# Tower kernel: unit turns by DMA in FFN block 0, down products by parts, block 1's attention rows by DMA

## The reference

```python
h = rms(rms(emb_table[x]) * norm_weight @ proj_weight.T)          # x: 16 x 256 token ids below 128
# attention, 16 heads of 32, on layernorm(h)
q, k = feature_map(u @ Wq.T), feature_map(u @ Wk.T); v = u @ Wv.T
attn = where(causal, (q k^T / sqrt(32)) ** 2, 0)
h = h + ((attn @ v) / (attn.sum(-1) + eps)) @ Wo.T
# FFN with Hadamard transforms (fwht), on layernorm(h)
x = fwht(x * SU_ug) / 64
a = silu(x @ W_gate.T * s_gate) * (x @ W_up.T * s_up)             # 512 -> 2048
h = h + fwht(a * SU_dp) / 64 @ W_down.T * s_down                  # 2048 -> 512
```

## Time and profile before

| | us |
|---|---|
| median of 3 runs | 1368.69 (1368.03 to 1368.8) |
| the profiled execution | 1369.22 |
| its span | 1367.4 |
| start to first `product` of block 0 | 0 to 64.5 |
| block 0's attention heads | 64.5 to 126.8 |
| output product, norm and mixing of block 0's rows | 126.8 to 168.3 |
| FFN block 0, gate and up | 168.3 to 324.1 |
| FFN block 0, down | 324.1 to 380.6 |
| FFN block 1 | 380.6 to 523.5 |
| FFN blocks 2 to 7 | 523.5 to 1367.4 |

### The profile page before, as it was taken

The page is one execution under the profiler, slowest core; times in us unless marked ns, Lnnn a source line. Parts: engine busy times, 40 slices in busy tenths (PEclk is TensorE's granted clock), DMA queues, the critical chain, the costliest instruction groups (busy, mean ns, idle before and its releaser), DMA issues.

```text
span 1367.4 us, 18781 instructions
## 1 busy us (share of the span) xinstructions
PE 1258.8 (92%) x7257; PEld 620.6 (45%) x7257; DVE 658.7 (48%) x1154; ACT 397.9 (29%) x703; POOL 565.2 (41%) x483
## 2 busy tenths in 40 slices
PE   5565398999999999999999999999999999999999
PEld 3453054554444444444444444444444444444444
DVE  2654558782645363545455445534553644361110
ACT  5452354442133212330233113311331133211210
POOL 0443244342266424752375227632664266421210
PEclk9797699999999999999999999999999999999999
DMA  9912313311435234423444244333543445020000
GB/s 307 318 24 62 78 36 65 70 26 37 100 101 109 47 93 108 106 57 85 101 108 70 70 101 108 83 67 90 115 86 55 100 101 108 16 70 24 0 0 31
DMA packets 232708, 113.97 MB, mean 83 GB/s; under 512 B 197893, under 2 KB 215609, under 8 KB 232121
## 3 DMA queue, kind: packets, MB, share of 16 engines
q1 hardware_dynamic: 220160, 74.38, 25.7%
q0 software_dynamic: 11520, 37.76, 9.4%
q10 hardware_dynamic: 952, 0.75, 0.2%
HBM read 57.01 MB, written 9.70 MB: 49 GB/s over the span
## 4 chain that ended last, share of the span: by engine, by line
PE 77%; DVE 9%; DMA 4%; issue 4%; ACT 4%; POOL 1%; SPq 0%; DVEq 0%; POOLq 0%; ACTq 0%
PE bank L1178 23%; PE bank L1179 23%; PE bank L1180 23%; PE bank L1330 3%; DMA prod<-sg 2%; PE bank L1173 2%; DVE wd L568 1%; PE bank L1221 1%; DVE wd L567 1%; DVE wgu L553 1%; DVE prod L765 1%; PE bank L1171 1%; DMA hid<-in_L_tok_norm_weight 1%; PE bank L1339 1%; ACT wgu L951 1%
## 5 line engine op out<-in xcount | busy, mean ns | idle before, releaser
L1178 PE MATMUL bank<-xT,wgu 128*128 128x512 f16 x1024 | 389.8, 381 | 1.4 <-DVE xT L804 1.4
L1179 PE MATMUL bank<-xT,wgu 128*128 128x512 f16 x1024 | 389.8, 381 | 0.0
L1180 PE MATMUL bank<-xT,wgu 128*128 128x512 f16 x1024 | 389.8, 381 | 0.0
L470 POOL TENSOR_TENSOR hid<-a,hid 128x512 f16<-128x512 f32 x128 | 172.9, 1350 | 284.4 <-ACT hid L951 284.1
L839 DVE SCALAR_TENSOR_TENSOR a<-bank,kap,sg 128x512 f32<-128x512 f32 x128 | 96.1, 751 | 313.6 <-PE bank L1180 296.1
L1178 PE MATMUL bank<-wd,hid 128*128 128x512 f16 x512 | 194.1, 379 | 0.0
L1180 PE MATMUL bank<-wd,hid 128*128 128x512 f16 x512 | 194.0, 379 | 0.0
L1179 PE MATMUL bank<-wd,hid 128*128 128x512 f16 x512 | 194.0, 379 | 0.0
L951 ACT ACTIVATE hid<-a 128x512 f16<-128x512 f32 x128 | 80.9, 632 | 278.8 <-DVE a L839 278.8
L1180 PEld LDWEIGHTS bank<-xT,wgu 128*128 128x128 f16 x1024 | 100.5, 98 | 121.9 <-issue 2.0
L1178 PEld LDWEIGHTS bank<-xT,wgu 128*128 128x128 f16 x1024 | 100.8, 98 | 117.7 <-DVE xT L804 2.3
(11 more groups left out here) (192 smaller groups left out, 1371.1 us busy)
## 6 DMA issues: line engine op xcount, KB each, us to landing
out<-a SPq DMA_DIRECT2D x24, 256.0 KB, 2.2
wgu<-in_L_ffn_W_gate SPq DMA_DIRECT2D x16, 256.0 KB, 6.6
wgu<-in_L_ffn_W_up SPq DMA_DIRECT2D x16, 256.0 KB, 5.1
wd<-in_L_ffn_W_down SPq DMA_DIRECT2D x4, 1024.0 KB, 9.3
out<-h_row SPq DMA_DIRECT2D x8, 256.0 KB, 2.0
hid<-att_table,ids_p POOLq DMA_INDIRECT x84, 3.5
xT<-in_L_tok_proj_weight SPq DMA_DIRECT2D x1, 1024.0 KB, 7.3
p<-in_L_attn_Wq SPq DMA_DIRECT2D x1, 1024.0 KB, 11.9
```

The lines of the kernel that those rows point to most:

```text
L470: nc.gpsimd.tensor_tensor(hid[:, 1, s, :], a32[:, :], hid[:, 0, s, :], ALU.subtract)\
L1178: mm(dst, w[0], v[0], start=first, stop=False)
L1179: mm(dst, w[0], v[1], start=False, stop=False)
L1180: return mm(dst, w[1], v[0], start=False, stop=final)
```

## The change

- A gate/up unit is now 128 rows by 512 columns. Units 0 to 11 are still turned by PE, beside block 0's attention, with a ring of three banks. Units 12 to 31 are made in slots 0 to 9 of block 0's FFN, two a slot, without PE: ACT scales the raw unit in place and copies its high part into one of three stage buffers (`RING = 3`), POOL makes the low part there, and SP issues one DMA transpose of both parts into the weights' tile. ACT waits with unit x until the transpose of unit x - 3 has landed.
- Down units go the same way, with DVE making the low part: split in slots 9 to 18, then PE multiplies by the float16 Hadamard matrix (two matmuls) in slots 10 to 22, ACT and DVE split the result.
- Block 0's gate and up have two banks each, as in the other blocks; the down product goes by four parts of the FFN columns, each part for all four row tiles.
- Block 0's attention takes 18 slots and a tail in place of 32. Its own attention rows and FFN input rows are now turned by PE (`o_flip`, `x_flip`) and copied by ACT. For block 1, whose attention runs in block 0's FFN, they stay with the DMA, now in one SP list with the units (`first_block`).
- Four butterfly passes go before block 0's FFN in place of two. The norm weights are loaded ahead of the projection's, the third down tile behind the gate and up weights.
- The value weights' turns move ahead of the score products; Wo's squares and turns move from before the first `product` into slots 4 to 7 and 13 to 16.

```diff
+RING = 3
+TURNED = 12
+UNIT_AT = tuple(range(1, 13))
+UNITS_BESIDE = 10
+DOWN_SQUARES = (3, 3, 3, 3, 2, 2)
+BOUND_BESIDE, FIT_BESIDE = 1, 6
+MIXED_BEFORE = 4
+MIX_BESIDE = (2, 3, 4, 5, 6, 7, 8, 8, 9, 10, 11, 12)
+SPLIT_BESIDE = (9, 10, 11, 13, 13, 13, 14, 14, 14, 15, 15, 15, 16, 16, 17, 18)
+HADA_BESIDE = (10, 11, 12, 14, 14, 15, 15, 16, 16, 17, 18, 18, 19, 20, 21, 22)
+NEXT_AT0 = (11, 13, 15, 17)
+HEADS_AT0 = (4, 8, 12, 16)
+O_AT0 = (5, 9, 13, 16)
+O_FLIP_AT0 = (6, 10, 14, 17)
+def units_beside(s):
+    return [TURNED + 2 * s, TURNED + 2 * s + 1] if s < UNITS_BESIDE else []
...
             def pair(b, s):
...
                 fetch(1, s)
                 feed(0, s)
+                for x in units_beside(s):
+                    unit_low(x)
                 product(1, s)
                 attend(1, s)
...
+            def unit_high(x):
...
+                if x >= TURNED + RING:
+                    act.wait_ge(*landed(x - RING))
...
+                if x < UNITS:
+                    act.wait_ge(S["gu_scaled"], x // 8 + 1)
+                    copy(unit_raw(x), unit_raw(x), scale=unit_scale(x)).then_inc(S["st_scaled"], 1)
+                    act.wait_ge(S["st_scaled"], x - TURNED + 1)
+                    copy(stage_of(x)[:, 0, :], unit_raw(x)).then_inc(S["st_hi"], 1)
...
-                feed(0, s, GATE0)
-                for u in units_beside(2 * s):
-                    unit(u, D_TURN)
...
+                feed(0, s, GATE[s % 2])
+                for x in units_beside(s):
+                    unit_high(x)
+                for v in down_hadas(s - 1):
+                    down_unit(v)
+                for v in down_splits(s):
+                    unit_high(UNITS + v)
                 feed_high(0, s)
...
+            def first_block():
+                for s in range(SUMS_AT[3] + 1):
+                    for x in units_beside(s) + [UNITS + v for v in down_splits(s)]:
+                        unit_turn(x)
+                    for q, m in P_TURN_AT.get(s, ()):
+                        p_turn(1, q, m)
...
+            def tail():
+                for m in range(4):
+                    row_sum(0, m)
+                    if m:
+                        x_low(0, m - 1)
+                    if m > 1:
+                        xT_low(0, m - 2)
+                    row_norm(0, m)
+                    if m == 0:
+                        pair_norm(2)
+                        half_terms(0)
+                    if m == 1:
+                        pair_scale(2)
+                        bound_low(0)
...
+                    if m == 3:
+                        pair_norm(3)
+                xT_low(0, 2)
+                x_low(0, 3)
+                down_mix(MIXED_BEFORE - 1)
+                xT_low(0, 3)
+                pair_scale(3)
...
+            def feed_down_by_parts(s):
+                part, m = (s - FT) // 4, (s - FT) % 4
+                if m == 0:
+                    pe.wait_ge(S["al_done"], 4 * part + 4)
+                    pe.wait_ge(S["d_lo"], 4 * part + 4)
```

More of the change, by code:

```diff
@@ L365, in _ @@
+            for m in range(4):
+                p_turn(1, 0, m)
+            first_block()
+            for b in range(1, NB - 1):
+                block_io(b, b + 1)
+            for m in range(4):
+                store(NB - 1, m)
             sp.wait_ge(S["stored"], 16 * 4 * NB)
@@ L1266, in _, with count @@
                 last.then_inc(S["qk_ready"], 1)
+            def count(n, bank):
+                for i in range(2):
+                    c = SEQ * i
+                    tokens = onehot0 if first(n) else onehot
+                    mm(bank[:, c:c + SEQ], tokens[:, 2 * i, :], cum0, start=True, stop=False)
+                    last = mm(bank[:, c + P:c + SEQ], tokens[:, 2 * i + 1, :], cum1, start=False, stop=True)
+                last.then_inc(S["count_ready"], 1)
+            pe.wait_ge(S["par_land"], PARAMS)
+            pe.wait_ge(S["onehot_ready"], 2)
+            count(0, COUNT0)
+            pe.wait_ge(S["wv_diag"], 2)
+            for u in range(12, 16):
+                small_unit(u)
             def qk_turn(i):
@@ new lines, in attend, with x_flip @@
+                if s in mix_at:
+                    x_mix(n, mix_at.index(s))
+                if s in wo_at:
+                    wo_rows(n, wo_at.index(s))
+            def x_flip(m):
+                pe.wait_ge(S["xl_done"], m + 1)
+                pe.wait_ge(S["xc_done"], m)
+                bank = PICK[0][:, :].bitcast(F16)
+                for i in range(2):
+                    for k in range(DC):
+                        c = (DC * i + k) * P
+                        last = nc.tensor.transpose(bank[:, c:c + P], x16[:, i, k * P:(k + 1) * P], ident16)
+                last.then_inc(S["flip_ready"], 1)
@@ new lines, in wo_rows @@
+            def wo_rows(n, m):
+                if m == 0 and first(n):
+                    pe.wait_ge(S["oT_done"], QUADS)
+                    pe.wait_ge(S["wo_lo"], 4)
+                elif m == 0:
+                    pe.wait_ge(S["oT_land"], 16 * QUADS * n)
+                if m >= 2:
+                    pe.wait_ge(S["h1_done"], 4 * n + m - 1)
+                c = slice(m * P, m * P + P)
+                for k in range(DC):
+                    last = split_mm(WOUT[m % 2][:, :], [oT[:, k, i, c] for i in range(2)],
+                                    [wo_t[:, i, k, :] for i in range(2)], k == 0, k == DC - 1)
+                last.then_inc(S["wo_ready"], 1)
```

1066 lines of the change are left out of this document (567 added, 499 removed).

## The result

The changed kernel takes 1357.8 us, median of 4 runs (1356.54 to 1361.44). The kernel before took 1368.36 beside it. The ratio is 0.9929, 95% interval 0.9907 to 0.9951: faster by 0.7%, where 2.7% were forecast, and the time lies above the forecast's range (1306 to 1350). The profiled execution is the slowest of the four, 1361.44 us with a span of 1359.6, so stages read from it are together 3.6 us longer than in the median.

A forecast was written before the change was run, and what follows sets the result against it. Blocks from 380.6 us on are PE-bound and unchanged; only earlier work moves. First gate at 147 plus 195.8 for FFN block 0 starts block 1 at 342.8, 37.8 earlier: 1369.2 - 37.8 = 1331.4, forecast 1331, range 1306 to 1350.

The forecast's parts named there:

- Up to the first product: Kernel start to block 0's first attention product: starts at 49.5 us in place of 64.5, 15 us gained.
- Block 0's attention: First product to first output product: heads 11.5 us apart, one 18 us stall at POOL's second gather, output product at 107.
- G: Start of FFN block 0's first gate matmul: 147 us, 21 earlier, bounds 138 and 154.
- FFN block 0, slots 0 to 9: First gate to slot 9's `hid<-a`: 94.0 us, with 1.5 charged for passes in six loops and 12 for slot 8.
- The loop of 7.9: FFN block 0's early slots: waiting for a stage buffer's transpose makes one `hid<-a` follow another by 7.9 us.
- the ring has slack: Rival: DVE and POOL don't collide, slots 0 to 9 take 7.9 us or less, second gather not held; 1310 us, chance 0.21.
- slots 10 to 15 and down: Rest of FFN block 0: DVE, then PE, sets the slots; last `a` at 130.5 us, then 65.3 to block 1.
- F: Time from FFN block 0's first gate matmul to block 1's: 195.8 us, 16.5 less, bounds 179 and 209.
- One float32 product goes, 18 matmuls come: 65.3: Last `a` to block 1: 62.3 us before, less 0.9, plus 3.9, gives 65.3.
- By parts, stores bunch, PE hides it: End of FFN block 0: finishes about 3.6 us apart, last store 14 after slot 28, PE needing its bank 15.4 after.
- PE's clock falls: Rival: pauses in each slot drop PE to 1.2 GHz, a slot's work taking 10.4 us; 1346 us, chance 0.18.
- SP's one list: Rival: unit transposes queue behind attention transposes waiting for gathers, four bursts of 13 us; 1383 us, chance 0.04.

The follow-up runs named there:

- e4: The change with POOL's second to fourth gathers for block 1 later in block 0's attention and its tail: 1354.1 us.
- e2: The change with the twelve butterfly passes beside FFN block 0 cut to 16 elements a partition (result not kept): 1345.9 us.
- e7: The change with a ring of four places in place of three for the gate/up units: 1359.9 us.
- e8: The change with POOL's low parts of 20 gate/up units cut to 16 of 512 columns (result not kept): 1346.6 us.
- e3: The change with all down-unit work left out of FFN block 0 (result not kept): 1326.4 us.
- e5: The change with DVE's low parts of down units ahead of block 1's attention row in slots 18, 20 and 22: 1349.3 us.
- e1: The change with the down units' Hadamard products one slot later on PE (slots 11 to 22): 1359.4 us.
- c3: c2 with only the first three Hadamard products of down units one slot later: 1341.1 us.
- c2: The change with the edits of e4 and e5 together: 1345.0 us.
- c4: c2 with down unit 3 taken after 4, 5 and 6, at most two units a slot in slots 9 to 15, Hadamard products rescheduled: 1347.0 us.
- c5: c4 with one of slot 8's two butterfly passes kept there, the others a slot later, and the unit order adapted: 1346.0 us.
- e6: e1 with ACT's scaled halves of down units behind its copies of `a` and of block 1's product: 1361.8 us.
- e9: The change with both the ring of four (e7) and the short POOL low parts (e8): 1347.2 us.

## Why the prediction was wrong, step by step

- **Up to the first product**, 49.5 forecast, 51.83 measured: 2.3 us late. The score products began at 46.4 in place of 45.1 and took 2.1 us in place of 1.1; from their end to the first product it was 3.3, 3.2 forecast. The 15 us gained are 12.7.
- **Block 0's attention.** Heads were to follow at 11.5 (the terms add up to 11.7, a slip); they came at 12.6, 13.7 and 17.0. The stall at POOL's second gather is there, and e4 prices it at 3.1 us. The output product was 7.5 late; the first product is 2.3 of that, and the two distances between heads 3.3. The tail was 38.1, 40 forecast. G is 5.7 over in this execution, 4.9 over by the mean of nine.
- **FFN block 0, slots 0 to 9.** 94.0 forecast, 92.5 measured, and steps of 7.7 to 9.4 in slots 1 to 8. The number was right, in part by luck. The loop of 7.9 is borne out by e2 (8.0 with the passes short). But the 1.5 us charged to each of six loops were about half a microsecond over slots 1 to 8, and the slot with two passes took 13.6 in place of 12; the errors went against each other. "A ring replaces it" is not the whole pace either: with a ring of four the length stays. The rule I quoted from the Trainium skill, SBUF — State Buffer, Who interferes with whom, has the two engines exclude each other for a whole instruction. By that rule 1.5 us a loop looked like a surcharge; the trace agrees with the rule where the two took turns (1.64 and 1.53 for products of 0.69), but a wait can also span several of POOL's instructions: 6.21 us for an operation of 1.22 (e7).
- **The rival "the ring has slack"** is out: ACT stood for landings eight times in the change, and steps 2 and 3 fell to 6.3 once a fourth place was there (e7). That alone brought no time; with POOL's low parts short it was 11 us (e8).
- **The step that failed: slots 10 to 15 and down.** I worked it out as DVE's work in slots 10 to 12 and PE's work in slots 13 to 15, and added the down units as 32 matmuls (7 us) and a low part or two a slot. None of their waits was priced: their transposes behind the ring's in SP's list, their products in PE's list ahead of the next gate, their low parts behind rows in DVE's. Without them, the last `a` comes at 126.2 and F is 185.9 (e3), under the forecast of 130.5 and 195.8. With them, 142.6 and 220.0. They cost 34 us of F (31.4 by the medians), where the forecast had 9.9 above e3's F. The first `a` behind the wait in slot 10, that of slot 11, came at 111.6 in place of 104.8. Of the 24.2 us by which F missed, 11.6 are the low parts behind a row (e5; 8.5 by the medians). The last `a` was 12.1 late, and 9.2 of that go with the Hadamard products a slot later (e1), but e1 gained no time by it, and with the first three alone it was 2.4 of F and 3.9 of the time (c3 against c2). These prices don't add up to the miss by themselves: e2 and e8, which leave the down units alone, each took 13.6 from F as well, so what the ring, the passes and POOL delay, the down units wait for too.
- **"One float32 product goes, 18 matmuls come: 65.3"** for the last `a` to block 1. With DVE's order mended it is 65.9 (e5). The work was counted rightly, the list it stands in was not.
- **By parts, stores bunch, PE hides it**: right to within the 4 us that PE idles there in e3. The distances of 3.6 and 14 us are not shown.
- **PE's clock falls.** It did, 0.84 and 0.91, but as a result. After its 13.44 us of waiting PE made ten matmuls from 256.61 on at 0.43 us each and one at 0.30, some 2.2 us over the faster step, on the path. With fewer waits the clock came back (0.88 and 0.97 in e3). That it is small as a cause is shown for this place only. By the starts in the timelines, about 76 of PE's 512-column matmuls in FFN block 0 stood 0.43 us apart in place of 0.216, where the kernel before has 20 and e3 has 47: some 16 us against 4 and 10. How much of that lies on the path, no run tells.
- **SP's one list**: not as I put it, by gathers. In slot 9 it did matter: the first down unit's transpose stood behind two others, and the four of `p` (5.43 us) held back the second unit's to 259.18, which PE did not notice, as it came to that product at 263.99 only and didn't wait.

What stays open: c3's last `a` is at 138.4, 12.1 us after e3's, with only 5.9 and 2.0 us left as longest waits of its Hadamard products. How much of that is the work of the halves on ACT and DVE, and how much is ring, banks and POOL, c4 and c5 did not tell apart. Nor was it tried to take e1's loss in slot 15 to a cause: e6 only ruled out one order.

## What to carry to other kernels

When work is moved into a stage, cost it by each list that it stands in, not by its own duration: for every operation ask what its engine's list holds behind it while it waits. Here down units with 7 us of matmuls cost 31 to 34, and three lines of order gave 8.5 back. Opening a loop of waits wins nothing where the work that it lets through meets a resource about as full (e7). And a gain in an early slot counts only if the next fixed wait of the stage moves too: e1 brought the last `a` forward by 9.2 us and the end not at all.

## What the runs showed of the hardware

A row of POOL operations can keep DVE's two-input operation out until the row ends: 6.21 us for a 128x1024 operation of 1.22, 5.23 for a product of 0.69, 6.02 for an operation on one column (e7), and 4.40 with four POOL operations, two of them of 0.2 us (e9). It need not: in the change five POOL operations stood in a row from 195.69 to 204.17, DVE got a turn between them, and both were stretched, POOL's from 1.16 to 1.60, DVE's from 0.69 to 1.53 and 1.64, with 2.18 for the longest operation of a pass. POOL's operation took 2.06 for 1.16 where a DVE operation had begun ahead of it (at 245.26). The forecast had charged each meeting with 1.5 us.
